# Seven products of quarter blocks in place of eight in a two-layer graph network, with the block combinations made by VectorE

## The reference

```python
h = relu(layernorm(x))
x = x + adj @ (h * keep(u) / 0.9)          # layer 1; keep(u) = u >= 0.1
h = relu(layernorm(x))
x = x + adj @ (h @ W) + b                  # layer 2
```

## Time and profile before

| | us |
|---|---|
| median of 3 runs | 921.59 (921.55 to 923.07) |
| the profiled execution's own time | 920.12 |
| its span | 918.3 |
| TensorE matmul busy | 900.0 (98%) |
| VectorE busy | 234.5 (26%), 449 instructions |
| ScalarE busy | 42.8 (5%) |
| read from HBM | 360.74 MB, 395 GB/s over the span |

### The profile page before, as it was taken

One profiled execution on the slowest core, in us unless ns is written; L12 is line 12 of the kernel. 1 busy time (PEld: TensorE's weight loads), 2 busy tenths in 40 slices (PEclk: granted clock), 3 DMA queues, 4 the chain that ended last, 5 costly groups with the idle time before them and its releaser, 6 DMA issues.

```text
span 918.3 us, 10443 instructions
## 1 busy us (share of the span) xinstructions
PE 900.0 (98%) x4488; PEld 415.4 (45%) x4488; DVE 234.5 (26%) x449; ACT 42.8 (5%) x120; POOL 2.6 (0%) x13
## 2 busy tenths in 40 slices
PE   6799999999999999999999999999999999999998
PEld 5445444444444444444444444444444444444443
DVE  5364732323203202030303021030220300300334
ACT  3100000000000000000000000000000000000000
POOL 1000000000000000000000000000000000000000
PEclk9999999999999999999999999999999999999999
DMA  8999999999999999999999999989999999999993
GB/s 348 421 420 420 422 420 422 420 421 421 421 420 421 420 421 420 421 419 421 403 419 379 410 367 380 399 339 369 385 353 382 371 386 419 390 390 389 412 422 149
DMA packets 52909, 363.53 MB, mean 396 GB/s; under 512 B 5728, under 2 KB 6016, under 8 KB 10752
## 3 DMA queue, kind: packets, MB, share of 16 engines
q1 hardware_dynamic: 52800, 362.83, 97.5%
q0 software_dynamic: 64, 0.03, 0.0%
HBM read 360.74 MB, written 2.10 MB: 395 GB/s over the span
## 4 chain that ended last, share of the span: by engine, by line
PE 92%; DMA 5%; SPq 2%; issue 0%; DVE 0%
PE banks L720 45%; PE row_sums L695 37%; PE banks L714 6%; DMA blocks<-in_adj 5%; PE banks L730 3%; SPq L464 1%; PE row_sums L704 1%; PE banks L807 0%; PE finished L772 0%; PE row_sums L772 0%; SPq L447 0%; SPq L446 0%; DVE x L654 0%
## 5 line engine op out<-in xcount | busy, mean ns | idle before, releaser
L720 PE MATMUL banks<-blocks,features 128*64 128x512 f32 x1912 | 665.2, 593 | 0.0
L695 PE MATMUL row_sums<-blocks,features 128*64 128x512 f32 x1696 | 547.1, 592 | 1.5 <-DMA blocks<-in_adj 1.5
L720 PEld LDWEIGHTS banks<-blocks,features 128*64 128x64 f32 x1912 | 221.3, 137 | 215.6 <-issue 215.1
L695 PEld LDWEIGHTS row_sums<-blocks,features 128*64 128x64 f32 x1696 | 192.7, 137 | 201.6 <-issue 196.4
L617 DVE TENSOR_TENSOR acc<-acc,banks 64x512 f32<-64x512 f32 (+1 forms) x112 | 76.8, 686 | 597.9 <-PE banks L720 540.7
L714 PE MATMUL banks<-blocks,features 128*64 128x512 f32 x224 | 98.1, 592 | 0.1
L524 ACT ACTIVATE turned<-finished 32x128 f32<-32x128 f32 (+1 forms) x68 | 17.8, 262 | 790.3 <-DVE finished L584 789.1
L730 PE MATMUL banks<-blocks,features 128*64 128x256 f32 x240 | 54.3, 379 | 0.1
L714 PEld LDWEIGHTS banks<-blocks,features 128*64 128x64 f32 x224 | 30.6, 137 | 29.0 <-issue 28.8
L730 PEld LDWEIGHTS banks<-blocks,features 128*64 128x64 f32 x240 | 32.8, 137 | 21.7 <-issue 8.5
L704 PE MATMUL row_sums<-blocks,features 128*64 128x256 f32 x256 | 30.5, 382 | 7.1 <-DMA blocks<-in_adj 7.1
(11 more groups left out here) (48 smaller groups left out, 97.0 us busy)
## 6 DMA issues: line engine op xcount, KB each, us to landing
blocks<-in_adj SPq DMA_DIRECT2D x339, 1024.0 KB, 13.0
out<-x SPq DMA_DIRECT2D x7, 256.0 KB, 3.6
x<-in_x SPq DMA_DIRECT2D x1, 1024.0 KB, 10.9
acc<-in_u SPq DMA_DIRECT2D x1, 1024.0 KB, 12.9
blocks<-in_adj SPq DMA_DIRECT2D x2, 512.0 KB, 25.1
x<-in_x SPq DMA_DIRECT2D x1, 768.0 KB, 7.2
acc<-in_u SPq DMA_DIRECT2D x1, 768.0 KB, 8.8
x<-in_x SPq DMA_DIRECT2D x1, 256.0 KB, 3.1
```

Of the source, the lines that this page charges most:

```text
L695: return nc.tensor.matmul(row_sums[at, t.unit % 2, nodes], features[:, tile_of(k, j), 0:D], tile, start=first and t.n == unit_first[t.unit ...
L720: return nc.tensor.matmul(banks[at, t.sum.bank, nodes], features[:, tile_of(t.k, j), D:2 * D], tile, start=t.n == t.sum.first and j == t.t ...
```

## The change

The items `both` of block rows 4 to 15 become items `seven`: 90 of the 92. The block is taken as a 2 x 2 matrix of quarters (two halves of its nodes by two pairs of its tiles, 128 x 2 x 256 each), and the features as a 2 x 2 matrix (two pairs of tiles by the two layers). Their product, which takes eight products of quarters, is formed from seven (Winograd's form of Strassen's algorithm). Each product is two matmuls of 256 columns; 14 such matmuls, seven in each half of the array, make 3.5 steps.

For each `seven`, VectorE makes four combinations of features (128 x 128 elements each, in `mixed`) and four of quarters (128 x 512 each: three in `quarters`, the fourth in place in the block), in `make_quarters`. `mixed` and `quarters` have two sets, so the ones of the item after the next can be made when an item is done. The seven products of a whole row add up in four banks of their own (`SEVEN_BANKS`), and when the row's last `seven` is done `add_seven` adds them to `x1` and `acc` in 16 instructions of 64 x 256 (`TERMS`); that is layer 1 and layer 2 of that row's items. The next row's first `seven` waits for that.

Besides this the number of slots goes from 16 to 15, the banks for other sums from 4 to 2 once the first `seven` has come (6 before), the transposes go through `row_sums` and the finishing products through the banks of the sevens. The features and u arrive in two parts in place of three. The planner starts the sevens of a row 3 us into it and ends them 6 us before its end, puts the item of the newest column (`both(k + 1, k)`) first among the late ones, and loads for sevens are ordered two items earlier. Since the rows now hold less work, the planner moves some reloaded pairs to later rows.

```diff
 KEPT = 2
-SLOTS = 16
+SLOTS = 15
 AHEAD_ROWS, AHEAD_TO = 2, BLOCKS
-SUM_BANKS = 4
-STEP, BLOCK_LOAD, LANDING, MARGIN, H2_LEAD, ROW_LEAD = 0.858, 2.49, 1.6, 8.0, 8.0, 10.0
-PARTS = [(0, 1), (1, 4), (4, PAIRS)]
+SEVEN_FROM = 4
+SEVEN_LOAD, SEVEN_MADE, SEVEN_SETS = 2, 3, 2
+SUM_BANKS, SEVEN_BANKS = 2, 4
+STEP, BLOCK_LOAD, LANDING, MARGIN, H2_LEAD, ROW_LEAD, SEVEN_OFF = 0.858, 2.49, 1.6, 8.0, 8.0, 10.0, (3.0, 6.0)
+PARTS = [(0, PAIRS // 2), (PAIRS // 2, PAIRS)]
 PART_OF = [n for n, (p0, p1) in enumerate(PARTS) for _ in range(p0, p1)]
+TERMS = [(1, 0, 0, 0, 1), (1, 1, 0, 0, 1), (2, 0, 0, 0, 1), (2, 1, 0, 0, 1),
+         (1, 0, 1, 0, 1), (1, 1, 2, 1, 1), (2, 0, 2, 1, 1), (2, 1, 2, 1, 1),
+         (1, 1, 3, 0, 1), (2, 0, 1, 1, 1), (2, 1, 3, 0, 1),
+         (1, 1, 3, 1, 1), (2, 0, 2, 0, 1), (2, 1, 3, 1, 1),
+         (1, 1, 0, 1, -1), (2, 1, 1, 1, 1)]
...
-        self.steps = 2 if kind == "one" else len(tiles)
+        self.steps = 2 if kind == "one" else 3.5 if kind == "seven" else len(tiles)
...
-        return Item("both", [self.operand(s, k)], k, s, s + 1)
+        return Item("seven" if s >= SEVEN_FROM else "both", [self.operand(s, k)], k, s, s + 1)
...
             late.append(Item("mix", [self.operand(k, k), other.operands[0]], k, k + 1, k + 2))
             late[-1].k1 = other.k
+        if 0 < k < BLOCKS - 1:
+            late.append(self.both(k + 1, k))
         for p in range(PAIRS - 1, -1, -1):
             if 2 * p + 1 <= k:
                 if stays(2 * p, k):
...
-        if 0 < k < BLOCKS - 1:
-            late.append(self.both(k + 1, k))
...
-                items += merged([both, ones, again, late], ROW_LEAD)
+                items += merged([both, ones, again, late], [SEVEN_OFF, (0, 0), (0, 0), (ROW_LEAD, 0)])
...
+    sevens = [t for t in items if t.kind == "seven"]
+    loads.sort(key=lambda load: load.first - (SEVEN_LOAD if items[load.first].kind == "seven" else 0))
...
+    released = -1
+    for load in loads:
+        released = max(released, load.before.until if load.before else -1)
+        load.released = released
+    for n, t in enumerate(sevens):
+        t.nth, t.set = n, n % SEVEN_SETS
+        t.at = max(t.n - SEVEN_MADE, t.loads()[0].released, sevens[n - SEVEN_SETS].n if n >= SEVEN_SETS else 0)
...
+        if q.seven is not None:
+            q.before = q_before or max((r for r in bank_of[SUM_BANKS:] if r), key=lambda r: r.done)
+            q_before = q
+            continue
+        q.bank = min(range(SUM_BANKS if q.last >= sevens[0].n else len(bank_free)), key=lambda b: bank_free[b])
+        quarters = sb("quarters", [P, SEVEN_SETS, 3, TILES // 2, HALF_BLK])
+        mixed = sb("mixed", [P, SEVEN_SETS, 4, TILES // 2, D])
...
-        finished = ctx.enter_context(nc.psum_tensor("finished", [P, 2, BLK], f32))
+        banks = ctx.enter_context(nc.psum_tensor("banks", [P, SUM_BANKS + SEVEN_BANKS, BLK], f32))
...
+            at = SUM_BANKS + n % 2 * 2
+            return banks[:, at:at + 2, :]
...
-                    dve.wait_ge(sum_added, ahead_done[s])
-                link2(nc.vector.tensor_tensor(sums_of_row, sums_of_row, row_sums[0:D, m % 2, 0:width(m)], ALU.add))
-                nc.vector.tensor_tensor(sums_of_row, sums_of_row, row_sums[D:P, m % 2, 0:width(m)], ALU.add)\
-                    .then_inc(row_summed, 1)
-                dve.wait_ge(row_summed, m + 1)
+                    dve.wait_ge(sum_added, max(ahead_done[s], seven_done.get(s, 0)))
+                for half in unit_last[m]:
+                    row_steps[0] += 1
+                    found = row_sums[half * D:(half + 1) * D, m % 2, 0:width(m)]
+                    nc.vector.tensor_tensor(sums_of_row, sums_of_row, found, ALU.add).then_inc(row_summed, 1)
+                    dve.wait_ge(row_summed, row_steps[0])
...
-                nc.vector.transpose(squares[x1_half(s), 0:width(m)], sums_of_row).then_inc(row_turned, 1)
+                nc.vector.transpose(row_sums[x1_half(s), m % 2, 0:width(m)], sums_of_row).then_inc(row_turned, 1)
...
+            def make_quarters(t):
+                a11, a12, a21, a22 = (quarter(t, nodes, tiles) for nodes in range(2) for tiles in range(2))
+                b11, b12, b21, b22 = (features_of(t, tiles, layer) for tiles in range(2) for layer in (1, 2))
+                t1, t2, t3, t4 = (mixed[:, t.set, n, :, :] for n in range(4))
+                dve.wait_ge(h2_ready, t.needs)
+                if t.nth >= SEVEN_SETS:
+                    dve.wait_ge(used, sevens[t.nth - SEVEN_SETS].n + 1)
+                nc.vector.tensor_tensor(t1, b12, b11, ALU.subtract).then_inc(seven_mixed, 1)
+                nc.vector.tensor_tensor(t3, b22, b12, ALU.subtract).then_inc(seven_mixed, 1)
+                dve.wait_ge(seven_mixed, 4 * t.nth + 1)
+                nc.vector.tensor_tensor(t2, b22, t1, ALU.subtract).then_inc(seven_mixed, 1)
+                dve.wait_ge(seven_mixed, 4 * t.nth + 3)
+                nc.vector.tensor_tensor(t4, t2, b21, ALU.subtract).then_inc(seven_mixed, 1)
+                s1, s2, s4 = (quarters[:, t.set, n, :, :] for n in range(3))
+                dve.wait_ge(block_arrived[t.loads()[0].slot], t.loads()[0].arrived)
+                nc.vector.tensor_tensor(s1, a21, a22, ALU.add).then_inc(seven_made, 1)
+                dve.wait_ge(seven_made, 4 * t.nth + 1)
+                nc.vector.tensor_tensor(s2, s1, a11, ALU.subtract).then_inc(seven_made, 1)
+                dve.wait_ge(seven_made, 4 * t.nth + 2)
+                nc.vector.tensor_tensor(s4, a12, s2, ALU.subtract).then_inc(seven_made, 1)
+                nc.vector.tensor_tensor(a21, a11, a21, ALU.subtract).then_inc(seven_made, 1)
+            def add_seven(q):
+                dve.wait_ge(used, q.last + 1)
+                done = {}
+                for n, (layer, nodes, bank, half, sign) in enumerate(TERMS):
+                    dve.wait_ge(sum_added, q.earlier + done.get((layer, nodes), 0))
+                    done[layer, nodes] = n + 1
+                    at = q.half if layer == 2 else 1 - q.half
+                    to = (acc if layer == 2 else x1)[at * D:(at + 1) * D, q.p, nodes_of(nodes)]
+                    nc.vector.tensor_tensor(to, to, banks[half * D:(half + 1) * D, SUM_BANKS + bank, 0:HALF_BLK],
+                                            ALU.add if sign > 0 else ALU.subtract).then_inc(sum_added, 1)
...
+                for t in sevens:
+                    if t.at == n:
+                        make_quarters(t)
...
+            def seven(t):
+                a11, a12, s3, a22 = (quarter(t, nodes, tiles) for nodes in range(2) for tiles in range(2))
+                s1, s2, s4 = (quarters[:, t.set, n, :, :] for n in range(3))
+                b11, b12, b21, b22 = (features_of(t, tiles, layer) for tiles in range(2) for layer in (1, 2))
+                t1, t2, t3, t4 = (mixed[:, t.set, n, :, :] for n in range(4))
+                opens, closes = t.n == t.sum.first, t.n == t.sum.last
+                def product(bank, half, of, by, j, only=False):
+                    return nc.tensor.matmul(banks[half * D:(half + 1) * D, SUM_BANKS + bank, 0:HALF_BLK], by[:, j, :],
+                                            of[:, j, :], start=opens and (only or j == 0),
+                                            stop=closes and (only or j == 1))
+                def products(bank, left, right):
+                    for j in range(2):
+                        product(bank, 0, *left, j)
+                        product(bank, 1, *right, j)
+                pe.wait_ge(seven_mixed, 4 * t.nth + 4)
+                products(0, (a11, b11), (a22, t4))
+                pe.wait_ge(seven_made, 4 * t.nth + 1)
+                products(1, (a12, b21), (s1, t1))
+                pe.wait_ge(seven_made, 4 * t.nth + 3)
+                products(2, (s4, b22), (s2, t2))
+                pe.wait_ge(seven_made, 4 * t.nth + 4)
+                product(3, 0, s3, t3, 0, only=True)
+                return product(3, 1, s3, t3, 1, only=True)
...
-                if m is not None and m >= 2 and t.n == min(unit_first[m]):
-                    pe.wait_ge(row_summed, m - 1)
+                if m is not None and m >= 2 and t.n == min(unit_first[m].values()):
+                    pe.wait_ge(row_placed, (m - 1) * (P // SQ))
+                    pe.wait_ge(row_placed_act, (m - 1) * (P // SQ))
...
-                    pe.wait_ge(row_summed, UNITS)
-                    pe.wait_ge(row_placed, UNITS * (P // SQ))
-                    pe.wait_ge(row_placed_act, UNITS * (P // SQ))
+                    pe.wait_ge(sum_added, max(seven_done.values()))
```

More of the change, by code:

```diff
@@ L245, in plan @@
             load.until = n
+    sevens = [t for t in items if t.kind == "seven"]
+    loads.sort(key=lambda load: load.first - (SEVEN_LOAD if items[load.first].kind == "seven" else 0))
     free, holder, count = [-1] * SLOTS, [None] * SLOTS, [0] * SLOTS
-    for load in loads:
+    for n, load in enumerate(loads):
         load.slot = min(range(SLOTS), key=lambda q: free[q])
```

(17 more changed lines are left out.)

51 lines of the change are left out of this document (29 added, 22 removed).

## The result

The changed kernel takes 943.82 us (median of 4 runs, 942.96 to 944.89), against 921.57 us for the kernel before beside it. The ratio is 1.0243, with a 95% interval from 1.0222 to 1.0264. The profiled execution took 943.57 us, its span 941.8 us.

What follows compares the result with a forecast made beforehand. TensorE's work bounds the kernel before; afterwards VectorE holds it back at row ends. 918.3 - 38.6 + 4.3 + 57.8 = 941.8 us span, 943.6 execution, about 945 with the median's 1.5; range 925 to 966 us.

Steps and rivals of the forecast that it cites:

- VectorE's two lumps: At each row's end, add_seven and the layer norm chain, 13.25 us together, precede the combinations TensorE needs next.
- TensorE's saving: In the 90 changed items, 4 steps become 3.5, with smaller matmuls at full rate: 38.6 us less.
- The other parts of the change: One slot less, features in two parts, the row_placed wait and transposes in row_sums: each taken as 0.
- The loads' share: TensorE's waits for blocks, added item by item along the planner's list, grow by 4.3 us.
- the price of 2.49 us for each load: In the sum of loads, a block of 1.05 MB at 421 GB/s takes 2.49 us.
- VectorE's price: VectorE needs 3.8 us for a seven's combinations in make_quarters and 7.0 us for add_seven.
- The waits: At the ends of rows 7 to 15, TensorE waits 57.8 us for combinations, h2_ready or banks.
- The clock's rival: TensorE's clock falls in the new pauses, adding 12 to 20 us, about 960 us in all; chance 22%.
- Busy time: Sign to look for: VectorE busy at about 660 us or more, near 100% at rows 12 to 15.
- The fast rival: VectorE is quick enough, quarter operations at 0.57 us, waits 28 us: 915 us, faster than before; chance 9%.

Runs made afterwards that it cites:

- eight: The changed kernel with eight products and no combinations, in the same items, order, slots, banks and loads: 923.73 us, ratio 1.0044 to the kernel before.
- no_make: The changed kernel without make_quarters (no combinations of features or quarters) and without TensorE's waits for it: 899.10 us, ratio 0.9769 to the kernel before.
- off_10_10: The changed kernel with a row's sevens starting 10 us into it and ending 10 us before its end, not 3 and 6: 929.86 us, ratio 1.0112.
- gp_features: The changed kernel with the four combinations of features made by GpSimd in place of VectorE: 936.98 us, ratio 1.0190 to the kernel before.
- filled2: The changed kernel with spare matmuls ahead of all waits of six sevens that followed TensorE's pauses: 940.59 us, ratio 1.0226 to the kernel before.

## Why the prediction was right, and where it was lucky

The forecast was 945 us, 941.8 of it span; measured were 943.8, and a span of 941.8. The sign and the place are shown, and so is the cause, VectorE's two lumps at the rows' ends ahead of the combinations: the same work spread out is 12 to 14 us faster, and without the combinations the kernel is 44 to 45 us faster. That the number fits to 1 us is in part luck, since terms were off both ways.

- **TensorE's saving, 38.6 us: right.** `eight` against `no_make` gives 38.3, and the matmuls of 256 columns keep their rate.
- **The other parts of the change, taken as 0: 4 us in `eight`.** The prediction put the slot, the parts of the features and the banks' new waits at nothing. Waits for blocks explain 0.8 us of the 4 (9.4 against 8.6).
- **The loads' share, 4.3 us: right for this order, wrong as a rule.** Waits for blocks rose by 4.8 us. With VectorE out of the way they rise by 10.2 (`no_make`), and with the lumps hidden pairs alone wait 17.8 us (`off_10_10`). The step that is wrong as a rule is the price of 2.49 us for each load everywhere.
- **VectorE's price: slightly high.** I had 3.8 us a seven and 7.0 for `add_seven`; measured are 3.6 and 6.75. The instructions of 512 elements take 0.69 us, as the row of L548 had it. Free neighbours do overlap, as the earlier trace rows showed: the features' combinations of 0.28 us start 0.20 us apart. The Trainium skill ("VectorE: DVE Perf Modes", The DRAIN you can't avoid) has an operation wait until the pipe is empty, except that one which is not held starts earlier; the trace agrees.
- **The waits, 57.8 us: of the right kind, too high by about 8.** With the measured distances the same sum gives about 50, my estimate, which the expectation of `gp_features` also uses. The profile shows 38.9 us as pauses. Pauses are counted from the modelled ends of matmuls, so they read short: at the end of row 14 three of them make 9.0 us where 10.2 were lost. The rest would lie in items that wait between their products, as the ones of 302 and 303 do (0.40 us from start to start at 811.22 and 815.53, where 0.22 is usual); its sum is not measured.
- **The clock's rival, 12 to 20 us at 22%: half right.** The clock did fall, six times, after pauses of 2.0 to 7.1 us. The array time lost was 11 us, near the price of 12 to 20; but filling the pauses, which returned 6 of the 11, gave back 1.6 to 3.2 us. That fits the reason given against the rival, that VectorE is the bound just then. The Trainium skill ("TensorE: Matmul & The Clock Gate", Why this matters for your kernels) has the clock go to half after idle gaps between matmuls; the trace agrees in kind, though pauses of 2.5 and 2.75 us passed without a fall.
- **What is open.** With the measured distances the sum is 8 us short of the span. The other parts of the change account for 4 of these if they cost here what they cost in `eight`, and the clock for 1.6 to 3.2. VectorE itself also stood 6.2 us waiting for blocks in `make_quarters`, with its other work queued behind. That these add up so is likely, but no run isolates them within the changed kernel.
- **Busy time.** I named 660 us for VectorE; 617.0 are shown, since overlapped instructions count once (their durations add up to 658.5). The same sign had "near 100%" for rows 12 to 15, and this failed: VectorE is busy for 79 to 82% of them. It had time to spare even there, but not at the place where TensorE waited, which speaks for the lumps once more.
- **The fast rival** (quarter operations under 0.6 us) is refuted by L671 to L677.

The change's named part is a loss of its own size: VectorE in place of GpSimd costs 5 to 7 us (ratios 1.0243 and 1.0190, medians 943.8 and 937.0).

## What to carry to other kernels

When work is moved to an idle engine, add it up per stage, and then look at what stands in that engine's program order in front of the instruction that the bound engine waits for. VectorE had some 20% of the last rows to spare and still could not hide two lumps of 6 to 7 us at their ends. Moving items by a few us, with the loads moved to match, was worth as much (24 to 25 us) as having the four feature combinations done for nothing (25 to 26 us). When the first bound shrinks by 4%, the second must be priced anew: a transfer rate read where many loads are queued doesn't hold where only two or three are under way.

## What the runs showed of the hardware that was not expected

- GpSimd and VectorE slow each other when both read SBUF with two operands: 0.45 us alone and 0.8 to 0.9 beside the other for GpSimd's, 0.69 and 0.82 to 0.94 for VectorE's. The mean over the kernel rose from 0.69 to 0.76 us, 0.80 for the in-place one.
- The 16 transfer engines can show a share of 0.97 at 355 GB/s, where 1.01 went with 421 GB/s when many loads were queued. With three blocks of 1 MB under way they show 0.99 at 396 GB/s in `off_10_10`; it took five for the full rate.
- After a pause of 2.0 us (at 616 us in the changed kernel) or 2.3 to 2.4 us (at 250 us in `eight` and `filled2`) the granted clock fell to 0.5 (1.2 GHz), while pauses of 2.75 us (683 us) and 2.5 us (891 us) in the changed kernel passed without a fall. At half clock the pairs of matmuls with 256 columns started 0.43 to 0.45 us apart in place of 0.21. Of the 6 us of array time that `filled2` returned, a quarter to a half showed in the kernel's time.
